# Attention block on one core: the diagonal quarter of each 32x32-block shuffle is issued by ScalarE's DMA queue instead of SyncE's

## The reference

```python
xf = x.reshape(b, -1, c)                    # 16 x 1024 tokens x 512
h = _group_norm(xf, norm_scale, norm_bias)  # 32 groups
qkv = h @ qkv_w + qkv_b                     # 512 -> 1536
q, k, v = jnp.split(qkv, 3, axis=-1)
# a plain reshape to (bs*8, length, 64): a "head" is a run of 128 tokens
weight = softmax(einsum('btc,bsc->bts', q*scale, k*scale))
a = einsum('bts,bsc->btc', weight, v)
h = a.reshape(bs, length, -1) @ proj_w + proj_b
return (xf + h).reshape(b, *spatial, c)
```

## Time and profile before

| | |
|---|---|
| Runs | 3977.83, 3987.15, 3997.38 us; median 3987.15 |
| The profiled execution's own time | 3982.65 us |
| Its span, first to last instruction | 3980.9 us, so 1.75 us lie around it |
| PE busy | 3704.3 us, 93% |
| ACT busy / POOL busy / DVE busy | 50% / 48% / 70% |
| DMA engines, mean busy share | 7 to 8 tenths in nearly all 40 slices |
| Mean granted TensorE clock | 0.988 of full speed |

### The profile page before, as it was taken

How to read it: one execution, slowest core, us unless ns; L and a number is a source line. 1 busy time by engine, 2 the same in 40 slices (tenths; PEclk the granted TensorE clock), 3 DMA queues, 4 the chain that set the end, 5 groups by cost and what they waited for, 6 DMA issues and landing times. The chain is left out here.

```text
span 3980.9 us, 77103 instructions
## 1 busy us (share of the span) xinstructions
PE 3704.3 (93%) x24128; PEld 2817.2 (71%) x24128; DVE 2789.2 (70%) x3473; ACT 1979.0 (50%) x3729; POOL 1928.3 (48%) x3274
## 2 busy tenths in 40 slices
PE   5999999999999999999999999999999999999997
PEld 4677777777777776767777777777777777777675
DVE  3777767677677776767767777776767767777665
ACT  3555455454554554545545555544545455455442
POOL 3454454454544544544545445445455454554451
PEclk9999999999999999999999999999999999999998
DMA  3778777777777777777777777777777777777776
GB/s 100 185 178 200 179 180 193 173 185 185 178 188 180 187 183 173 187 181 185 180 181 180 184 191 174 188 180 182 192 173 186 182 175 194 176 183 189 169 173 162
DMA packets 284584, 715.96 MB, mean 180 GB/s; under 512 B 77968, under 2 KB 77968, under 8 KB 284048
## 3 DMA queue, kind: packets, MB, share of 16 engines
q1 hardware_dynamic: 254224, 638.35, 66.5%
q10 hardware_dynamic: 29824, 71.32, 7.0%
HBM read 71.84 MB, written 33.55 MB: 26 GB/s over the span
## 5 line engine op out<-in xcount | busy, mean ns | idle before, releaser
L656 DVE TENSOR_REDUCE neg_max<-s_ps 128x1 f32<-128x1024 f32 x1024 | 1243.8, 1215 | 1022.5 <-PE s_ps L387 1020.9
L518 ACT ACTIVATE probs<-s_ps,neg_max 128x1024 f32<-128x1024 f32 x1024 | 1143.0, 1116 | 1383.1 <-DVE neg_max L656 1373.7
L637 DVE STREAM_TRANSPOSE turned<-probs 128x1024 f32<-128x1024 f32 x1024 | 1263.6, 1234 | 28.7 <-DMA probs_t<-turned 22.1
L418 PE MATMUL pv_ps<-probs_t,v 128*64 128x256 f32 x8192 | 989.9, 384 | 17.8 <-DMA probs_t<-turned 15.0
L418 PEld LDWEIGHTS pv_ps<-probs_t,v 128*64 128x64 f32 x8192 | 561.9, 137 | 302.4 <-issue 68.8
L458 PE MATMUL c_ps<-h_hi,w_hi 128*128 128x256 f32 x2048 | 591.4, 289 | 119.2 <-ACT crossed L534 105.8
L787 POOL CAST attn_hi<-attn 128x256 fp32r<-128x256 f32 x256 | 101.5, 396 | 1150.0 <-DVE attn L650 583.3
L459 PE MATMUL c_ps<-h_lo,w_hi 128*128 128x256 f32 x2048 | 578.7, 283 | 0.0
L460 PE MATMUL c_ps<-h_hi,w_lo 128*128 128x256 f32 x2048 | 577.6, 282 | 0.0
L458 PEld LDWEIGHTS c_ps<-h_hi,w_hi 128*128 128x128 f32 x2048 | 388.4, 190 | 187.5 <-ACT crossed L534 148.5
L530 ACT ACTIVATE staged<-c_ps,qk_bias 128x256 f32<-128x256 f32 x512 | 241.5, 472 | 431.5 <-POOL q_e L764 218.5
(11 more groups left out here) (77 smaller groups left out, 6113.8 us busy)
## 6 DMA issues: line engine op xcount, KB each, us to landing
probs_t<-turned SPq DMA_DIRECT2D x4096, 128.0 KB, 2.4
x_res<-in_x SPq DMA_DIRECT2D x128, 256.0 KB, 2.7
result<-x_res SPq DMA_DIRECT2D x128, 256.0 KB, 2.3
x_next<-in_x SPq DMA_DIRECT2D x120, 256.0 KB, 2.9
kh_e<-kh_e ACTq DMA_DIRECT2D x64, 256.0 KB, 3.4
kh_o<-kh_o ACTq DMA_DIRECT2D x64, 256.0 KB, 4.8
kl_e<-kl_e ACTq DMA_DIRECT2D x64, 256.0 KB, 5.6
kl_o<-kl_o ACTq DMA_DIRECT2D x64, 256.0 KB, 7.1
```

The lines of the kernel that those rows point to most:

```text
L418: last = nc.tensor.matmul(pv_ps[side][CH * par:CH * (par + 1), 0, :], v_sb[:, ring_of(i, parity), CH * chunk:CH * (chunk + 1)], p_t[:, par ...
L518: nc.scalar.activation(probs[k % 2][:, :], s_ps[k % 2][:, :], ACT.Exp, bias=neg_max[:, k % 4:k % 4 + 1], accum_out=row_sum[:, (k // HALF) ...
L637: nc.vector.transpose(dst, probs[(k - 1) % 2][:, :].rearrange("p (k b j) -> p k b j", k=CHUNKS, b=QUADS)).then_inc(probs_turned, 1)
L656: nc.vector.tensor_reduce(neg_max[:, k % 4:k % 4 + 1], s_ps[k % 2][:, :], AX.X, ALU.max, negate=True).then_inc(max_ready, 1)
```

## The change

`move_half` on SP leaves out `step == 0`, the four diagonal copies. ACT gets a new function `move_diagonal`, with the same two waits and the same four copies, and the same semaphores count them. ACT calls it in the same slots (1, 5, 9, 13 of a pair), behind the slot's exponential and ahead of the slot's staging, and so in slot 13 ahead of `double_k`.

```diff
@@ move_half, on SP
                 at_least_aside(sp, pv_done, half - 1)
-                for step in range(QUADS):
+                for step in range(1, QUADS):
                     for a in range(QUADS):
                         to = (a + step) % QUADS
@@ on ACT
+            def move_diagonal(b, k):
+                n = (k - MOVE_LAG) // HALF
+                half = 2 * BLOCKS * b + n
+                act.wait_ge(probs_turned, HALF * half + HALF)
+                at_least(act, pv_done, half - 1)
+                for a in range(QUADS):
+                    act.dma_start(probs_t[n % 2][Q * a:Q * (a + 1), a, :],
+                                  turned[n % 2][Q * a:Q * (a + 1), a, :]).then_inc(moved[n % 2][a], 16)
+
@@ ACT's slot
                     softmax_exp(b, k)
+                if k % HALF == MOVE_LAG % HALF and within(s - MOVE_LAG, N_SLOTS):
+                    move_diagonal(b, k)
                 if kind == "qk" and within(made_pair(b, k), N_PAIRS):
```

## The result

| | before | after |
|---|---|---|
| Median of 4 runs, us | 3987.43 | 4386.5 (4381.22 to 4400.62) |
| Profiled execution, its own time, us | 3982.65 | 4381.22 |
| Span, us | 3980.9 | 4379.3 |
| Ratio of the runs | | 1.1006, 95% interval 1.0969 to 1.1043 |

The profile after. First the busy times of its page; the same row of before is the earlier trace rows.

The account below looks back on a forecast made before the run. PE, busy 93%, bounds the kernel, and the key copies' landing already decides when a pair starts. 3982.65 + 228 (keys) + 96 (clock) + 6 (slots 1, 5, 9) - 4 (half-moves) = 4309, said as 4310 us; range 4180 to 4410.

Parts of the forecast that it names:

- the forecast's case: In slot 13 the key copies queue behind ACT's diagonal copies and land later: 4310 us, 8% slower, chance 0.60.
- Waits of the new function, nothing: On ACT, both semaphores `move_diagonal` waits for are there already when ACT reaches it: no cost.
- Key copies late, 228 us: In slot 13 the keys land 4.1 us later behind 0.52 MB of diagonal copies, costing PE 228 us at pair starts.
- Clock, 96 us: Longer PE idling ahead of pairs drops the clock in 48 more pairs, 2.0 us each: 96 us.
- ACT held in slot 13: Eight issues instead of four delay slot 14's exponential to near 2192 from 2188.28 us, hidden by the key wait.
- Slots 1, 5, 9, 6 us: ACT's four issues there delay staging by at most 0.2 us in slot 5; taken as 0.1 us x 64 = 6 us.
- Half-moves earlier, minus 4: SP issues 1024 copies fewer, each half lands about 1 us earlier: minus 4 us, at best minus 15.
- larger share: Rival: q10 gets two thirds of 249 GB/s for the diagonal too, key shift 3.1 us: 4230 us, chance 0.22.
- ACT's issuing as the bound: Rival: slot 13's eight issues take 1.85 us each, 14.8 us, delaying the exponential and pair start: 4470 us, chance 0.12.
- the faster side: Rival: keys land as before and half-moves end earlier, gaining up to 15.0 us: 3968 us, chance 0.03.
- the signs: If right: `kl_o` waits some 250 us, landing 14 to 15.5 us behind SP's first issue; if wrong: `crossed` waits grow largely.

Follow-up runs that it names:

- Experiment 9: Changed kernel with ACT's diagonal copies only in slot 13, ahead of the key copies, each carrying 32 of 1024 numbers per partition: 4207.64 us, ratio 1.0556.
- Experiment 10: Kernel before, plus one DMA of 0.52 MB to HBM on ACT's queue ahead of each pair's key copies: 4193.62 us, ratio 1.0514.
- experiment 5: Changed kernel with 16 more matmuls on PE ahead of each pair's wait for the key copies: 4296.82 us, ratio 1.0791.
- experiment 6: Changed kernel with ACT's diagonal copies only in slot 13 and behind the key copies, SP doing all 16 elsewhere: 4058.11 us, ratio 1.0186.
- experiment 1: Changed kernel with ACT's diagonal copies only in slot 13, SP issuing all 16 in slots 1, 5 and 9: 4345.04 us, ratio 1.0899.
- experiment 8: Changed kernel with ACT's diagonal copies only in slot 1 of each pair: 4013.41 us, ratio 1.0075.
- experiments 4: Changed kernel whose diagonal copies of slot 13 carry 256 of 1024 numbers per partition: 4282.16 us, ratio 1.0741.

## Why the prediction was right, and where its sizes were off

The forecast was 4310 us, measured 4386.5, inside the range of 4180 to 4410, and the forecast's case came true: the keys queue behind the diagonal copies.

- *Waits of the new function, nothing:* right; no wait for `probs_turned` or `pv_done` shows on ACT.
- *Key copies late, 228 us:* 254 net. Forecast shift 4.1 us, measured 4.7, 4.7 and 4.2 us away from the loop's turn and 3.5 us at it. The size is near; the reason given for it was incomplete, and that the number came out is in part luck. It was worked out as the time of 0.52 MB at half of the rate, with nothing for the issues. Experiment 9 shows that the issues alone, 2.7 us in which ACT's stream has not come to `kh_e`, make 2.7 to 3.1 us of the shift, and the bytes on top of them 1.4 to 1.8. Experiment 10, with its bytes alone, has 2.4 to 3.0 us and not 4.1. In the sum the issue time had been priced for ACT (2.6 us), but not for the keys' landing.
- *Clock, 96 us:* 113 us of longer matmuls, and experiment 5 gets 90 us back by keeping PE busy. Right. The price of each drop was near the forecast's 2.0 us; in the three kinds of pairs away from the loop's turn the two slots behind the wait are 1.4, 2.1 and 1.9 us longer.
- *ACT held in slot 13:* right that it costs nothing here. In this order the exponential of slot 14 is done about when PE runs out of other work. In the other order the hold is longer, and experiment 6 puts it at 73 us, 1.2 us a pair.
- *Slots 1, 5, 9, 6 us:* the term that was mis-sized. It measured some 40 us in the changed kernel, both as growth of the waits of `c_ps` and as the difference to experiment 1, and 104 us when it stands alone. The step that failed read one pair, whose staging had 2.4 us of room, and took it for all. In slot 41 the room was 1.75 us and the issues took 4.2 instead of 2.6. For slot 1 it looked at ACT alone; what was hurt in experiment 8 was an x load of SP's and, for a reason not shown, the key copies of the fourth pair.
- *Half-moves earlier, minus 4:* the wait for `probs_t` fell from 15.0 to 8.4 us. Right, and as small as said.
- The rivals: q10 had no larger share while it served the diagonal, 0.44 of 0.96 MB; ACT's issuing as the bound did not decide, since the eight issues took 7.0 us (2406.16 to 2413.11) and not 14.8; the faster side was wrong.
- Of the signs, the wait for `kl_o` came out at 330.1 us and not some 250, `kl_o` landed 15.7 us behind SP's first issue at 2404.55 (14 to 15.5 were said), and the waits for `crossed` grew from 105.8 to 120.5 us where they were to stay.

The Trainium skill ("DMA: Bandwidth & Descriptors", section "Issuing engines are not separate DMA queues") holds that another issuer saves sequencer time and no more. The changed kernel agrees on the engines: 1.04 busy at 236 GB/s, no faster than the 249 GB/s of before. It adds what that costs: the time saved on SP, for whose copies PE had waited only 15 us, was spent on ACT, whose next DMAs PE waited for.

What stays open: why the four issues take 4.4 instead of 2.8 us in one kind of pair even when ACT's queue holds only 4 KB copies (experiment 9), while in the changed kernel `kh_e` comes 2.7 us behind the exponential there too; and what else than the length of the idle time decides whether the clock falls. It was not tried how the bytes' part divides between ACT's own queue and SP's; experiment 10 adds bytes rather than moving them.

## What to carry to other kernels

Before you spread DMAs over a second issuing engine, look at what already stands in that engine's queue. A copy with slack that is put ahead of one without slack passes its time on in two ways, by its bytes and by the issues that the engine must get through first; price both. Where a wait is decided by a landing, try to issue that DMA earlier in its own stream, which is where the 0.8% were here. When PE's idle time ahead of a stage grows from one or two us to over four, add the lower clock behind it as a term of its own; in between, these runs went either way.

## What the runs showed of the hardware beyond that

- Four copies of 32 partitions x 128 bytes took ACT's stream as long to issue as four of 32 x 4096 bytes: keys 2.8 us behind the exponential at best in both (experiments 1 and 9). One copy of 128 partitions and 0.52 MB, to HBM, took 0.34 us (experiment 10). In these runs the price of an issue did not follow its bytes.
- With both queues filled, nearly all of it copies of SBUF to SBUF, the DMA engines were full at 236 GB/s (1.04 busy); with SP alone it was 210 GB/s at 0.92.
- The granted clock fell to its lower level after 1.98 us of PE idle time in experiment 5, and stayed up after 1.60 us in the earlier trace rows and after 3.38 us at 2254.48 us of the kernel before. In experiments 4 and 9 most second pairs of a batch idled 2.5 to 2.9 us and kept the full clock, while a few lost it after 2.5 or 2.6 us. What else decides is not shown.
